# ScalarE's ReLUs of a step's first two taken tiles, moved between the two halves of the chunk's ReLU

## What is computed

```
e = edge_attr @ We + be                       # one number per edge times a row of 512
m = relu(x[src] + e)                          # 40,000 rows of 512
agg = segment_sum(m, dst, num_segments=N)     # edges are sorted by dst
h = ((1.0 + eps) * x + agg) @ W1 + b1
h = batch_norm(h) ; h = relu(h)
x = relu(h @ W2 + b2)
```

## Time and profile before

| | |
|---|---|
| median of 3 runs | 1721.02 us (1719.23 to 1727.67) |
| profiled execution, first to last instruction | 2011.5 us, granted PE clock 0.887 |
| PE busy | 1575.7 us, 78% |
| DVE busy | 1309.7 us, 65% |
| POOL busy | 1027.9 us, 51% |
| ACT busy | 971.1 us, 48% |
| chain that ended last | PE 49%, DVE 19%, issue 11%, an unknown queue 9%, ACT 8% |

### The profile page before, as it was taken

The page is one execution under the profiler, slowest core; times in us unless marked ns, Lnnn a source line. Parts: engine busy times, 40 slices in busy tenths (PEclk is TensorE's granted clock), DMA queues, the critical chain, the costliest instruction groups (busy, mean ns, idle before and its releaser), DMA issues.

```text
span 2011.5 us, 22868 instructions
## 1 busy us (share of the span) xinstructions
PE 1575.7 (78%) x7214; PEld 688.0 (34%) x7214; DVE 1309.7 (65%) x2538; ACT 971.1 (48%) x1262; POOL 1027.9 (51%) x1070
## 2 busy tenths in 40 slices
PE   2767788869787787876888887877967887777968
PEld 1223333335442222332433232333423322324445
DVE  7667777776675676755585666675565775665644
ACT  3434444434435565554436556564345664564411
POOL 3766665665144566655056666662246665651033
PEclk8887888978889888988889998999888988989979
DMA  7655655665265566655166666662456665663733
GB/s 254 189 167 159 178 169 162 177 217 160 72 193 172 170 185 182 185 162 154 53 209 171 194 197 183 188 203 82 126 172 197 195 190 169 186 190 105 265 130 115
DMA packets 119099, 343.30 MB, mean 171 GB/s; under 512 B 20712, under 2 KB 24892, under 8 KB 118718
## 3 DMA queue, kind: packets, MB, share of 16 engines
q0 software_dynamic: 85248, 278.41, 47.8%
q1 hardware_dynamic: 32318, 60.78, 9.3%
q10 hardware_dynamic: 1408, 2.56, 0.5%
HBM read 323.61 MB, written 19.96 MB: 171 GB/s over the span
## 4 chain that ended last, share of the span: by engine, by line
PE 49%; DVE 19%; issue 11%; another core or an unknown queue 9%; ACT 8%; DMA 2%; DVEq 1%; POOL 1%; ACTq 0%; POOLq 0%
PE ps L1902 44%; DVE ring L1075 9%; ACT ring L1681 5%; PE ps L1975 3%; DVE lg L1131 2%; ACT zT L1726 1%; DVE aggT L1495 1%; DVE onehot L1066 1%; PE ps L2060 1%; ACT parts L1690 1%; DVE aggT L1132 1%; DVEq L1118 1%; DMA aggT<-pair_table,token_i 1%; DMA zT<-pair_table,token_i 0%
## 5 line engine op out<-in xcount | busy, mean ns | idle before, releaser
L878 POOL DMA_INDIRECT ring<-x_table,idxT x1014 | 985.4, 972 | 799.7 <-issue 274.7
L1075 DVE SCALAR_TENSOR_TENSOR ring<-ps,wT,ring 128x512 f32<-128x512 f32 x930 | 627.5, 742 | 7.3 <-issue 2.0
L1681 ACT ACTIVATE ring<-ring 128x1536 f32<-128x1536 f32 (+1 forms) x313 | 463.2, 1514 | 200.1 <-DVE ring L1075 141.0
L1902 PE MATMUL ps<-ring,onehot 128*32 128x512 f32 x2028 | 417.9, 683 | 102.9 <-ACT ring L1681 48.3
L1902 PE MATMUL ps<-ring,zT 128*128 128x512 bf16 x1080 | 298.8, 403 | 154.9 <-issue 105.1
L1726 ACT ACTIVATE zT<-ps 128x512 f32<-128x512 f32 x336 | 194.3, 599 | 366.6 <-PE ps L1902 206.8
L1131 DVE TENSOR_REDUCE lg<-ps 128x128 f32<-128x512 f32 x208 | 142.9, 687 | 288.2 <-PE ps L1975 127.6
L1902 PE MATMUL ps<-zT,xT 128*32 128x512 f32 (+2 forms) x752 | 221.2, 691 | 0.0
L1902 PEld LDWEIGHTS ps<-ring,zT 128*128 128x128 bf16 x1080 | 97.7, 100 | 303.0 <-issue 162.1
L1902 PEld LDWEIGHTS ps<-ring,onehot 128*32 128x32 f32 x2028 | 87.6, 118 | 312.4 <-issue 253.3
L1902 PE MATMUL ps<-aggT,w 128*128 128x256 f32 (+2 forms) x512 | 154.9, 455 | 13.1 <-DVE aggT L1132 9.6
(11 more groups left out here) (328 smaller groups left out, 1408.3 us busy)
## 6 DMA issues: line engine op xcount, KB each, us to landing
ring<-x_table,idxT POOLq DMA_INDIRECT x1014
zT<-slot_table SPq DMA_DIRECT2D x36, 312.5 KB
w<-in_L_gnn_W SPq DMA_DIRECT2D x8, 1024.0 KB
ring<-in_L_ffn_W SPq DMA_DIRECT2D x16, 512.0 KB, 9.7
x_table<-ring SPq DMA_DIRECT2D x24, 250.0 KB
x_table<-ring SPq DMA_DIRECT2D x9, 256.0 KB
stage<-in_x ACTq DMA_DIRECT2D x9, 256.0 KB
pair_table<-mix SPq DMA_DIRECT2D x9, 256.0 KB
```

Source lines behind the costliest of these rows:

```text
L878: gp.indirect_dma_start(out=to, out_offset=None, in_=table[:, :], in_offset=bass.IndirectOffsetOnAxis(ap=idx, axis=0)).then_inc(done, 16)
L1075: ins = v.scalar_tensor_tensor(out=at[:, u, :], in0=terms[:, :], scalar=wT[:, c, u:u + 1], in1=at[:, u, :], op0=ALU.mult, op1=ALU.add)
L1681: a.activation(at, at, ACT.Relu).then_inc(relu_done, 1)
L1902: return nc.tensor.matmul(o, lhsT, rhs, start=start, stop=stop)
```

## The change

In the whole steps of the mixed layers ACT does the ReLUs of the step's first two taken tiles behind the first half of the chunk's ReLU and ahead of its second half. Before, they stood behind `parts_copy`, `beside` and `early_copy`. Sorted chunks have one part only, so there the two ReLUs stand behind it and ahead of `parts_copy`. Nothing is added or removed, and no wait's value is changed.

```
+            def relu_part(l, j, p):
+
+                part = parts_of(l, j)[p]
+                a.wait_ge(summed, l_sums(l, j) + p + 1)
+                at = rows_of(l, j)[:, part.start:part.stop, :]
+                a.activation(at, at, ACT.Relu).then_inc(relu_done, 1)
+
             def relu(l, j):
 
-                for p, part in enumerate(parts_of(l, j)):
-                    a.wait_ge(summed, l_sums(l, j) + p + 1)
-                    at = rows_of(l, j)[:, part.start:part.stop, :]
-                    a.activation(at, at, ACT.Relu).then_inc(relu_done, 1)
+                for p in range(len(parts_of(l, j))):
+                    relu_part(l, j, p)
...
+                    first, later = tiles_of(l, j) if l in MIXED else ([], [])
                     if l not in MIXED or j > 1:
-                        relu(l, j)
+                        relu_part(l, j, 0)
+                        pick_relus(l, first)
+                        for p in range(1, len(parts_of(l, j))):
+                            relu_part(l, j, p)
+                    else:
+                        pick_relus(l, first)
                     parts_copy(l, j - 1)
                     beside(l, j)
                     early_copy(l, early_of(l, j - 1))
                     if l in MIXED:
-                        first, later = tiles_of(l, j)
-                        pick_relus(l, first)
                         if copy_at(j) is not None:
                             pick_copy(l, copy_at(j))
                         pick_relus(l, later)
```

## The result

The changed kernel takes **1776.93 us** (median of 4 runs, 1769.81 to 1780.12), the kernel before 1720.40 us (4 runs beside them, 1719.23 to 1727.67). The ratio is 1.0306, 95% interval 1.0271 to 1.0341: slower by 3.1%, or 53 to 57 us. The forecast was slower, 1758 us, with a range of 1710 to 1812.

A forecast was written before the change was run, and what follows sets the result against it. No engine is full; the order of waits between engines sets the pace, PE nearest to full. 45 steps x 0.97 us of delay = 44 us, 2.2% of the profiled span, so 1721 x 1.022 = 1758 us, range 1710 to 1812.

The forecast's parts named there:

- the forecast's own bounds: Mixed loops: 25 to 65 steps delayed by 0.97 us each, 24 to 63 us, scaled to 1741 to 1775 us.
- PE waits for the second half: Mixed steps: PE loads second-half weights right on ACT's end, within 0.12 us in 65 of 98 steps paired.
- Work between the halves: Mixed steps 4 to 36: two tile ReLUs delay the second half by 0.97 us; 45 steps counted, 44 us.
- of the 40 between, I take half: Mixed steps where PE starts on ACT's end but the chain skips the second half: half counted, PE having half the chain.
- 25 steps of the chain for 24 us: Mixed loops: the chain passes through a whole second half 25 times, each losing 0.97 us; at least 24 us.
- slower by more: Between the halves: ACT also stands still for PE's takes, 71 us, half felt; 80 us in all, 1789 us; chance 0.20.
- Hidden by the ring: Mixed loops: POOL gathers up to four chunks ahead, so PE's delay comes from slack; 1721 to 1727 us; chance 0.24.
- Banks come free earlier: Mixed steps: earlier tile ReLUs let PE's later takes start sooner; 15 us gained at most, 1708 us; chance 0.14.
- parts_copy, side jobs, steps 1 to 3 at nothing: ACT's copies and side jobs move back 0.97 us, their readers 7 to 10 us away; early steps lack second halves: nothing.
- Scaling by the spans' ratio: Whole kernel: 44 of 2011.5 us profiled, 2.2%, applied to the timed 1721 us, if waits shrink as the whole does.

The follow-up runs named there:

- e0_before: The kernel before the change, unaltered, run again for a profile on a slower chip: 2048.45 us.
- f0_change: The changed kernel, unaltered, run again on a slower chip against the kernel before: 2124.9 beside 2041.9 us, ratio 1.0378.
- e3_behind_second_half: Kernel before, with the first two tiles' ReLUs directly behind the second half, ahead of `parts_copy` and side jobs: ratio 1.0059, or 0.999 by medians over all runs.
- e2_waits_only: Kernel before, with ACT waiting between the halves for both takes and a buffer, tiles' ReLUs at their old place: 2105.2 beside 2039.2 us, ratio 1.0303.

## Why the prediction was right, point by point

The direction and the mechanism (PE waits for the half that is pushed back) were right. The size is in part luck: as far as the experiments show, the forecast's own term, work, was put too high (44 us against 10 to 20, or at most 29 with the clock taken out), the waits were left out of it, and the two errors have opposite signs. 1776.9 lies 2 us above the forecast's own bounds of 1741 to 1775 and inside the range only because that reached up to the rival's case.

- **PE waits for the second half, so pushing it back costs.** Right, and shown: the same mechanism appears in the rows of every kernel that pushes it back. I read PE on ACT's end in 65 of 98 steps (75 of 102 pairs in e0_before); after the change it was in all 102. A delay makes its own steps critical, so the count before is no upper bound for the count after.
- **Work between the halves, 45 x 0.97 = 44 us.** The size failed. I let 45 of 99 steps count, a share of 0.45. Measured on chips like the profiled one, work alone is felt at 0.11 to 0.21, and 99 x 0.97 = 96 us of it would be about 10 to 20 us (29 at most, by the 0.30 with the clock taken out). The step that failed is "of the 40 between, I take half", and the lower bound, 25 steps of the chain for 24 us, was by those runs already slightly too high. What is on the chain is not lost in full; PE's later waits shrink by a part of it. On the first chip the split was not measured.
- **The waits for takes.** I put them in a rival, "slower by more", at half of 71 us, and gave it 0.20. They belonged in the forecast: on chips like the profiled one they are the larger part, +3.0 and +3.4% against +0.5 to +0.9% for work (at least 46 us against at most 26, with the clock taken out as above). That rival's sum, 36 + 44 = 80 us of 2011.5 or 4.0%, is close to the 3.8% measured there (its terms are not: about 65 us for waits, 10 to 20 for work, so that the agreement is luck). The reason I gave against it was that late signals may be of the profiled execution alone. They were there on all three chips of the experiments. For the first chip the reason was right: the changed kernel's trace has no wait at all that ended on "remote", where f0_change has 151 with 550 us in total. But it did not carry: ordinary waits for takes still make 85 of the 181 us of delay there.
- **Why 3.1% there.** If work is felt at 0.20 and waits at 0.34, about as in the table, 96 and 85 us give 19 + 29 = 48 us, against 53 to 57 measured. This is worked out, not shown: none of the experiments ran on a chip with 1720 us, so the split between work and waits there stays open.
- **Hidden by the ring.** Refuted. In the changed kernel POOL still waited for PE at `ring` 92.9 us in 53 places, even on the quicker chip. In f0_change it waited 341.3 us in 80 against 219.1 in 60 in e0_before; with the waits put down to "remote" it is 420.6 against 355.0, so it rose by 66 us.
- **Banks come free earlier.** Refuted as a gain: the 91 us by which PE's waits at takes fell did not win against the 157 us it lost, and e3_behind_second_half, which gives the banks early without touching the second half, isn't faster. The Trainium skill (Perfetto Trace Analysis, "Optimizing Scalar/DVE Operations") says that breaking up instructions on an engine that isn't full, but causes bubbles elsewhere, may let work finish sooner. Nothing was broken up here, so the case does not test that sentence. Work put into a break that was there already cost 3.1%, with ACT 55% busy after.
- **parts_copy, side jobs, steps 1 to 3 at nothing.** No run isolated it. e3_behind_second_half pushes the same instructions back and came out between 0.999 and 1.006, with what the banks gave in it.
- **Scaling by the spans' ratio.** The ratio carried over roughly: +3.8% on a 2042 us chip and +3.1% on the 1720 us chip. The waits behind it are not the same kind on the two, so this is no rule.

## What to carry to other kernels

Ask of an instruction that is moved ahead not how long it runs, but what it waits for and who needs what stands behind it: on the f chip the waits that came with two ReLUs of 0.97 us cost about four times what their running did (+3.4 against +0.9%), or about twice with the clock taken out. Be wary of a wait for engine A in front of a result that A needs and that is ready without it: here one such wait a step cost 2.2%, and two and a buffer's 3.0 to 3.4%. And a delay of an instruction on the critical path need not be felt in full: here a ninth to a third of it reached the end, in part because the delayed engine then waited less elsewhere.

## What the runs showed of the hardware

The same program took 17 to 20% longer in the experiments than in the runs of the result, and I put this down to the chip. The kernel before took 1720.4 us (4 runs) on the first chip and 2009.5 (7 runs) to 2041.9 (16 runs) on others; the changed one 1776.9 and 2124.9. It is not the clock alone: the granted clock was 0.952 in the profiled execution of the changed kernel there, and 0.888 in that of f0_change. By (1 - clock) x span that is 85 against 238 us, so the clock makes at most 153 of the 346 us between the two spans. What differs as well is how long other engines wait for PE. DVE's wait for PE's fold (L1131), in the list of waits of the changed kernel on the first chip and then of the same kernel in f0_change (us in total, times, longest):

```profile
DVE lg L1131 <- PE ps L1984: 103.5, 102, 2.6
```

```profile
DVE lg L1131 <- PE ps L1984: 235.6, 88, 10.9
...
DVE lg L1131 <- remote: 95.9, 31, 7.3
```

That is a mean of 1.0 us in 102 waits against one of 2.8 us in 119, for the same instructions. Over all engines no wait on the first chip is put down to "remote"; in f0_change 151 are, 550 us in total, in e0_before 197 with 685 us, and in the profile shown before 189 with 577 us. In the rows of f0_change above a take that ended at 712.78 by the model let ACT go only at 719.88. The granted clock was full over most of that stretch, 1.00 from 711.3 to 718.9, and fell to half of it (the lower of its two levels, 0.50) at 719.0, until 725.8. Whether the signal or the matmul itself was late, and what held it up, no row shows. In practice: where a profile has waits of this kind, expect a wait between engines to cost several us now and then (here up to 6.8 us ahead of the second half in e2_waits_only), however short the work behind it is.
